# GNN megakernel: the attention layer in 13 parts of 32 edge tiles from one ring of gathered rows

## What is computed

```python
h = (x @ W).reshape(n, 8, 32)
a_src, a_dst = einsum(h, att_src), einsum(h, att_dst)      # n x 8
e = leaky_relu(a_src[src] + a_dst[dst], 0.2)               # edges and one loop per node
m = segment_max(e, dst); e = exp(e - m[dst])
out = segment_sum(h[src] * (e / segment_sum(e, dst)[dst]), dst)
x = layernorm(x + gamma * norm(out + bias) + beta)
```

## Time and profile before

| | us |
|---|---|
| runs shown (3) | 2991.97, 2983.28, 2981.79; median 2983.28 |
| profiled execution, span from first to last instruction | 2974.2 |
| busy: PE, DVE, ACT, POOL | 2470.6, 1396.0, 707.2, 936.7 |

### The profile page before, as it was taken

The page is one execution under the profiler, slowest core; times in us unless marked ns, Lnnn a source line. Parts: engine busy times, 40 slices in busy tenths (PEclk is TensorE's granted clock), DMA queues, the critical chain, the costliest instruction groups (busy, mean ns, idle before and its releaser), DMA issues. The chain is left out here.

```text
span 2974.2 us, 32381 instructions
## 1 busy us (share of the span) xinstructions
PE 2470.6 (83%) x9483; PEld 1621.2 (55%) x9484; DVE 1396.0 (47%) x3940; ACT 707.2 (24%) x1552; POOL 936.7 (31%) x927
## 2 busy tenths in 40 slices
PE   3677789897987999999999999999977886457680
PEld 2444788343766555565556555577743444345560
DVE  7999656455665001030101001455575664546668
ACT  3776545111443000010001000255400000103112
POOL 0000256666666000000000000012167666576740
PEclk9888999998998999999999999999988998678885
DMA  6565678343344743444444434333558887646641
GB/s 233 243 253 225 212 238 264 118 138 97 112 121 137 152 151 129 151 134 151 129 152 133 151 119 145 93 106 102 113 168 271 278 282 245 209 132 190 192 127 43
DMA packets 209534, 493.89 MB, mean 166 GB/s; under 512 B 46457, under 2 KB 128430, under 8 KB 209134
## 3 DMA queue, kind: packets, MB, share of 16 engines
q1 hardware_dynamic: 135185, 301.30, 32.2%
q10 hardware_dynamic: 38173, 133.27, 12.8%
q0 software_dynamic: 36032, 57.60, 7.1%
HBM read 374.71 MB, written 117.32 MB: 165 GB/s over the span
## 5 line engine op out<-in xcount | busy, mean ns | idle before, releaser
L794 POOL DMA_INDIRECT table_dense_weights<-pair_weight,dst x416 | 411.2, 988 | 563.5 <-DVE weights_c L849 324.8
L1526 PE MATMUL banks<-own_term,features_and_rows 128*128 128x391 f32 (+1 forms) x1656 | 552.3, 491 | 0.0
L2134 POOL DMA_INDIRECT features_and_rows<-table_heads,src x376 | 401.7, 1068 | 191.4 <-issue 107.9
L1526 PEld LDWEIGHTS banks<-own_term,features_and_rows 128*128 128x128 f32 x1656 | 312.2, 189 | 226.8
L1552 DVE TENSOR_SCALAR features_and_rows<-banks,hop_bias 128x391 f32<-128x391 f32 (+1 forms) x24 | 15.0, 625 | 762.2 <-PE banks L1526 762.2
L954 PE MATMUL banks<-split_rows,count_columns 128*128 128x512 f32 x1200 | 322.1, 415 | 19.6 <-issue 12.6
L2531 PE MATMUL banks<-features_and_rows,edge_to_window 128*128 x880 | 233.4, 427 | 104.5 <-DVE edge_to_window L2492 71.6
L1526 PE MATMUL banks<-features_and_rows 128*128 128x391 f32 (+1 forms) x840 | 282.4, 491 | 0.0
L954 PEld LDWEIGHTS banks<-split_rows,count_columns 128*128 128x128 f32 x1200 | 226.3, 193 | 76.8 <-issue 21.7
L2531 PEld LDWEIGHTS banks<-features_and_rows,edge_to_window 128*128 128x128 f32 x880 | 181.3, 210 | 156.5 <-issue 122.5
L558 PE MATMUL banks<-features_and_rows,pair_and_bias_rows 128*128 128x400 f16 x806 | 184.3, 388 | 87.1 <-DVE features_and_rows L540 51.9
(11 more groups left out here) (425 smaller groups left out, 3016.8 us busy)
## 6 DMA issues: line engine op xcount, KB each, us to landing
hidden<-table_counts SPq DMA_DIRECT2D x305, 160.0 KB
table_dense_weights<-weights_c ACTq DMA_DIRECT2D x26, 1600.0 KB, 5.7
own_term<-table_dense_weights SPq DMA_DIRECT2D x52, 782.0 KB
features_and_rows<-table_rows_by_edge SPq DMA_DIRECT2D x58, 528.0 KB
own_term<-table_dense_weights SPq DMA_DIRECT2D x34, 780.5 KB
pair_and_bias_rows<-table_edge_rows ACTq DMA_DIRECT2D x50, 512.0 KB
weights_c<-table_edge_rows ACTq DMA_DIRECT2D x50, 512.0 KB
table_rows_by_edge<-features_and_rows SPq DMA_DIRECT2D x48, 528.0 KB
```

The source lines that it names most:

```text
L794: e.indirect_dma_start(out=self.table, out_offset=bass.IndirectOffsetOnAxis(ap=self.place[:, t:t + 1], axis=0), in_=self.values[:, t:t + 1 ...
L1526: m = e.matmul(psum[b][:, 0:wide], z_block(block)[:, f * P:(f + 1) * P], streamed[tile % STREAM][:, lo - from_column:lo - from_column + wi ...
L2134: e.indirect_dma_start(out=to[:, k, :], out_offset=None, in_=t_h, in_offset=bass.IndirectOffsetOnAxis(ap=src[:, t:t + 1], axis=0)).then_in ...
```

## The change

- The 112 scoring stages, the index tables in DRAM, the staging, the write and gather of segment maxima, and the multiplication by own rows in ACT go.
- The head row gets 8 more columns (272 in the ring). The 33rd number of each head is now a_src itself instead of 1, so a gathered row brings its score.
- POOL gathers the 416 tiles in order into a ring of 80 tiles in SBUF, after the two first quads also two fetches of values at the first nodes of scan rows and parts. Then, on POOL too, the own rows are scaled and added to the node sums, in 7 groups of two operations (`add_own`).
- 13 parts of 32 tiles. For each: `prepare`, `weigh`, then `merge_dve`/`merge_pe`, written out instead of in a loop. A scan row is now 2 tiles of one head, so a part's scores are [128, 256]. The exponential is a polynomial on DVE; the weights are turned into PSUM and from there also put into the ring as the 33rd numbers. The own row's exponent comes out of the merge in the 8 new columns, and ACT makes its exponential at each node tile's end.
- A part's scan begins without knowing what follows: what a node that crosses a part bound still has behind it is found in advance. For each of the 12 bounds a round of one POOL fetch of 128 rows of counts (6,400 bytes each) and two DVE operations of 3,200 columns marks the sources of that node (`near_fetch`, `near_counts`), six rounds behind the evictions of hop 0 and six behind those of hop 1, and 12 rounds of small operations with them; a reduction over nodes at the start of the attention gives the bounds' maxima.
- Start values go to one table, one indirect write per node tile instead of two. SP loads dst rows for the scan after the last rows of the third layer, and begins that layer's counts only when the marks are known.
- `wait_loaded` replaces waits on a value from memory: it masks the register first.

The diff, cut to its core:

```diff
+RING_TILES = 80
+RING_AHEAD = 16
+RING_QUADS = RING_TILES // GROUP
+RING_ROW = ATT_ROW + HEADS
+PART_TILES = 32
+PARTS = EDGE_TILES // PART_TILES
+PART_EDGES = PART_TILES * P
...
+        def wait_loaded(e, sem, loaded, bound):
+
+            e.reg_alu(bound, loaded, 511, ALU.bitwise_and)
+            e.wait_ge(sem, bound)
...
-                e.wait_ge(s_zeroed, e.snap(regs[2 * n + 1], min_val=3, max_val=WINDOWS + 2))
+                wait_loaded(e, s_zeroed, regs[2 * n + 1], bound)
...
+        def near_fetch(b, known):
+            def pool(e):
+                if b == 0:
+                    for ready in (*written, known):
+                        e.wait_ge(*ready)
+                else:
+                    e.wait_ge(*near_read[b - 1])
+                e.indirect_dma_start(out=near_rows.rearrange("p k n -> p (k n)"), out_offset=None, in_=t_count,
+                                     in_offset=bass.IndirectOffsetOnAxis(ap=bound_at[:, b:b + 1], axis=0)).then_inc(s_near, 16)
+
+            pr.queue["pool"].append(pool)
+
+        def near_counts(b, ready):
+            t = V(lambda e: e.tensor_scalar(near_hot, iota[:, :], bound_low[:, b:b + 1], None, ALU.is_equal), ready)
+            t = V(lambda e: e.tensor_tensor(near_rows, near_rows, near_hot.unsqueeze(1).broadcast_to([P, NODE_TILES, P]), ALU.mult),
+                  (s_near, 16 * (b + 1)), t)
+            near_read[b] = V(lambda e: e.tensor_reduce(near_penalty[:, b, :], near_rows, AX_X, ALU.add), t)
+            return near_read[b]
...
             e.wait_ge(*w_h)
-            for n in range(STAGED):
-                d = n % DIRECT
-                if n >= DIRECT:
-                    e.wait_ge(s_kept_rows[d], 16 * (n // DIRECT))
-                gather_group(e, STAGED_QUADS[n], staging[d], s_staged[d], GROUP // 2 * n - STAGES_BEHIND)
-                if n == 3:
+            for quad in range(QUADS):
+                if quad >= RING_QUADS:
+                    e.wait_ge(*merged((quad - RING_QUADS) * GROUP + GROUP - 1))
+                for t in range(quad * GROUP, (quad + 1) * GROUP):
+                    e.indirect_dma_start(out=ring_rows[:, ring_at(t), 0:ATT_ROW], out_offset=None, in_=t_h,
+                                         in_offset=bass.IndirectOffsetOnAxis(ap=src[:, t:t + 1], axis=0)).then_inc(s_row[quad % RING_QUADS], 16)
+                if quad == 1:
                     e.wait_ge(*w_pair)
-                    e.wait_ge(*row_first_known)
+                    e.wait_ge(*row_first_in)
                     for c in range(2):
-                        e.indirect_dma_start(out=first_value[:, c:c + 1], out_offset=None, in_=t_pair,
-                                             in_offset=bass.IndirectOffsetOnAxis(ap=row_first[:, c:c + 1], axis=0)).then_inc(s_first_value, 16)
-            gather_direct(e, [q for q in DIRECT_QUADS if q < 2 * IN_CHAIN])
-            gather_direct(e, [q for q in DIRECT_QUADS if 2 * IN_CHAIN <= q < PLACES])
-            gather_last(e)
-            weigh_own(e)
...
+        def add_own(e):
+            for n, g in enumerate(node_groups):
+                rows_of, weights_of = own_rows(g)[:, :, :, 0:HEAD_DIM], tiles(p_self, g)
+                e.wait_ge(s_own_back[g[0] // 16], 16)
+                e.wait_ge(s_summed, g[-1] + 1)
+                e.tensor_tensor(rows_of, rows_of, weights_of.unsqueeze(3).broadcast_to([P, len(g), HEADS, HEAD_DIM]), ALU.mult
+                                ).then_inc(s_own_scaled, 1)
+                e.wait_ge(s_own_scaled, n + 1)
+                sums_of = sum_rows(g)[:, :, :, 0:HEAD_DIM]
+                e.tensor_tensor(sums_of, sums_of, rows_of, ALU.add).then_inc(s_owned, 1)
 
         pr.queue["pool"].append(gather_rows)
-        s_dst_rows = pr.sem("scan_dst_loaded")
...
+        def prepare(b):
+            before = pr.last("dve")
+            seg_made = V(lambda e: e.tensor_tensor(seg[:, 1:], by_dst[:, b, 0:LAST], by_dst[:, b, 1:], ALU.subtract), scaled_dst, before)
+            for c in range(2):
+                held_read[b] = V(lambda e, c=c: e.tensor_tensor_scan(held_in[:, c, :], seg, psum[4][:, c * SCAN_LEN:(c + 1) * SCAN_LEN],
+                                                                     first_value[:, b, c:c + 1], ALU.add, ALU.max),
+                                 held_turned[b], (s_first_value, 32), seg_made)
+            V(lambda e: e.tensor_scalar(begins_here, start_values[b % 2][:, :, :, 0], -0.1 * BIG, None, ALU.is_gt), (s_start[b % 2], 16 * (b // 2 + 1)))
+            V(lambda e: e.tensor_scalar(flags[:, 0, :], by_dst[:, b, :], by_dst[:, b, 0:1], -1.0, ALU.subtract, ALU.mult), scaled_dst)
+            V(lambda e: e.tensor_scalar(flags[:, 1, :], by_dst[:, b, :], by_dst[:, b, LAST:], None, ALU.subtract))
+            for w in range(2):
+                V(lambda e, w=w: e.tensor_scalar(end_mask[:, w, 2 * P:], bound_key, end_key[:, b, w:w + 1], -BIG, ALU.not_equal, ALU.mult))
+                masked_ends[b] = V(lambda e, w=w: e.tensor_scalar(end_mask[:, w, 0:2 * P], keys_of, end_key[:, b, w:w + 1], -BIG,
+                                                                  ALU.not_equal, ALU.mult), keys_spread[b])
+            for j in range(2 * b, min(2 * b + 2, NODE_TILES)):
+                V(lambda e, j=j: e.tensor_tensor(x[:, j, :], x[:, j, :], brow[:, B_BETA, :], ALU.add))
...
+        def turn_scores(b):
+            landed = [row_landed(quad) for quad in part_quads(b)]
+            for lo, hi, at in pieces_of(b):
+                t = V(lambda e, lo=lo, hi=hi, at=at: e.tensor_copy(
+                    in_rows(packed, lo, hi), by_row(ring_rows[:, at:at + hi - lo, HEAD_DIM:ATT_ROW:HEAD_ROW])), *landed)
+            for i in range(SCAN_TILES):
+                m = T(lambda e, i=i: e.transpose(a_turned[:, i * P:(i + 1) * P], packed[:, i, :], ident[:, :]), t, masked_ends[b])
+            return m
+
+        def weigh(b):
+            m = turn_scores(b)
+            t = V(lambda e: e.tensor_tensor(met, a_turned, held_in[:, 1, :], ALU.add), m, held_read[b])
+            t = V(lambda e: e.scalar_tensor_tensor(out=bent, in0=met, scalar=0.2, in1=met, op0=ALU.mult, op1=ALU.max), t)
+            t = V(lambda e: e.tensor_tensor(met, bent, held_in[:, 0, :], ALU.max), t)
+            scanned = V(lambda e: e.tensor_tensor_scan(prefix, seg, met, -BIG, ALU.add, ALU.max), t)
+            V(lambda e: e.tensor_copy(back[:, LAST:], prefix[:, LAST:]), scanned)
+            spread_max = V(lambda e: e.tensor_tensor_scan(back[:, 0:LAST][:, ::-1], seg[:, 1:][:, ::-1], prefix[:, 0:LAST][:, ::-1],
+                                                          prefix[:, LAST:], ALU.add, ALU.max), scanned)
+            for w, at in enumerate((0, LAST)):
+                m = T(lambda e, w=w, at=at: e.matmul(end_values[:, w * P:(w + 1) * P], back[:, at:at + 1].broadcast_to([P, P]), ident[:, :],
+                                                     start=True, stop=True), spread_max)
+            t = V(lambda e: e.tensor_tensor(at_ends, end_mask, all_values.unsqueeze(1).broadcast_to([P, 2, ALL_KEYS]), ALU.add),
+                  m, masked_ends[b], bound_spread)
+            t = V(lambda e: e.tensor_reduce(end_value[:, :], at_ends, AX_X, ALU.max), t)
+            for w in range(2):
+                t = V(lambda e, w=w: e.scalar_tensor_tensor(out=back, in0=flags[:, w, :], scalar=end_value[:, w:w + 1], in1=back,
+                                                            op0=ALU.add, op1=ALU.max), t)
+            of_tiles = lambda to, i: to.rearrange("p (r i) h -> p i r h", i=SCAN_TILES)[:, i, :, :]
+            for i in range(SCAN_TILES):
+                max_turned = T(lambda e, i=i: e.transpose(of_tiles(max_of, i), back[:, i * P:(i + 1) * P], ident[:, :]), t)
+            gap = met
+            t = V(lambda e: e.tensor_tensor(gap, bent, back, ALU.subtract), t)
+            t = V(lambda e: e.tensor_scalar(power, gap, LOG2_E, -126.0, ALU.mult, ALU.max), t)
+            t = V(lambda e: e.tensor_scalar(rounded, power, ROUNDER, None, ALU.add), t)
+            scaled = V(lambda e: e.tensor_scalar(scale_i.bitcast(I32), rounded, ROUNDER - 127.0, float(1 << 23), ALU.subtract, ALU.mult), t)
+            t = V(lambda e: e.scalar_tensor_tensor(out=rest_of, in0=rounded, scalar=ROUNDER, in1=power, op0=ALU.subtract, op1=ALU.subtract), t)
+            t = V(lambda e: e.tensor_scalar(power, rest_of, EXP2[-1], None, ALU.mult), t)
+            for k in range(len(EXP2) - 2, 0, -1):
+                t = V(lambda e, k=k: e.scalar_tensor_tensor(out=power, in0=power, scalar=EXP2[k], in1=rest_of, op0=ALU.add, op1=ALU.mult), t)
+            t = V(lambda e: e.scalar_tensor_tensor(out=gap, in0=power, scalar=EXP2[0], in1=scale_i, op0=ALU.add, op1=ALU.mult), t, scaled)
+            for i in range(SCAN_TILES):
+                m = T(lambda e, i=i: e.transpose(of_tiles(weight_of, i), gap[:, i * P:(i + 1) * P], ident[:, :]), t)
+            own_gap = by_tile(rounded)
+            begins = start_values[b % 2][:, :, :, 0]
```

(38 more changed lines are left out.)

863 lines of the change are left out of this document (303 added, 560 removed).

## The result

Beside the kernel before on one chip (2987.2 us, median of 4), the changed kernel takes 3035.1 us (3027.8 to 3039.2, 4 runs): ratio 1.0148, 95% interval 1.0116 to 1.0180. It is slower by 1.5%, where 2875 us and faster had been forecast. The profiled execution's span is 3035.4 us against the 2866.2 of the sum. First the head of the page, and its chain by engine.

A forecast was written before the change was run, and what follows sets the result against it. Waits set the pace before; after the change POOL's gathers would. 2186.5 + 552.5 + 2.7 + 15.7 + 29.3 + 71.5 + 8 = 2866.2 us span, with 9.1 more 2875 us; range 2837 to 2936, 8 in 10.

The forecast's parts named there:

- Item 1: Start of POOL's gathers: stays at 2186.5 us, behind the last write of head rows.
- Item 2: POOL's 418 gathers and first-value fetches: 522.5 us plus 30 of stretching, 552.5 us in all, 42.5 per part of 32.
- the stretching: Gathers made longer beside DVE instructions with both inputs in SBUF: 30 us taken, bounds 0 and 50.
- the 24 of its working: Stretching beside the small SBUF operations of 12 parts, 1.9 us each: 24 us, with 6 more for set-up beside part 0.
- Item 3: DVE's chain in a part of the merge stretch: 38.6 us, under POOL's 42.5, so POOL is the bound.
- merge 18.0: Merge of a part's eight quads by DVE and PE, about two of them slow: 18.0 us of the part's 38.6.
- Item 4: After the last gather: landing 2.7 us, last part 15.7 and 29.3, last norm and rest to the span's end 71.5.
- Item 5: Own rows scaled and added on POOL near the end: 8 us taken, bounds 0 and 24.6.
- Item 6: Before 2186 us: twelve nearest-source rounds of 15 us fit DVE's idle time in the hops, cost 0; bounded waits also 0.
- The 9.1 us: Added to the summed span: the distance of the three runs' median, 2983.28 us, above the profiled span of before.
- A: Rival: DVE's chain bounds each part at P of 44 to 50 us; chance 0.25, including gathers that don't come free.
- The signs set for being wrong: The prediction is wrong if POOL's last gather comes after 2800 or the last norm starts after 2860.

The follow-up runs named there:

- e1: Changed kernel with the merge's matmuls reporting once in four steps instead of every step: 3016.7 us, ratio 1.0127 to the kernel before.
- e12: Changed kernel in its own order, with six small products of POOL after every 4 gathers: 3058.7 us, single run.
- e13: Changed kernel, next part weighed while one is merged, SP's 16 target-number transfers behind the table's last writes: 2744.2 us beside 2804.3, ratio 0.9791.
- e17: Changed kernel as it is, timed again beside the kernel before: 2765.5 us against 2802.7, ratio 0.9868.
- e16: Kernel before with bounded waits, POOL waiting after every 8 gathers for landed rows once the merge has begun: 2846.5 us beside 2804.3, ratio 1.0146.

## Why the prediction was wrong

- *Item 1, the start*: 2205.9, not 2186.5. 4.4 us go with hops that end 4.9 us later in this execution (1921.6 against 1916.7 for their last matmul; in e1 to e12 they end at 1900.4 to 1913.0, so this part isn't the change's), 15.0 from SP: "the start stays at 2186.5, behind the last write of head rows" counted POOL's queue and not SP's, on which 16 transfers of target numbers are moved ahead of the last two writes. e13 shows it (0.3 us). In e1 to e12 this wait is 12.3 to 16.8 us.
- *Item 2, gathers at 552.5 us*: right where TensorE isn't held up: 536.7 in e17 (418 x 1.25 is 522.5, and 8.8 are waits for PE; the stretching was 5, not 30; the 24 of its working are 22.8 by their own factors, 12 x 1.9). In the first profile 693.5.
- *Item 3, "POOL is the bound; DVE has 3.9 us spare"*: the failed step. The chain was sized roughly right, even too long (35.3 us without gathers, 38.6 forecast), and in e17 DVE waits 7.1 us a part for rows. But "merge 18.0" took PE's blocks at their recorded pace beside 24 gathers in a row, and two stalls of 11 and 5.5 us came on top. The part became 53.3 us long, DVE had nothing spare, and POOL waited for PE's merge (129.9 us put down to it, 42.3 more to "remote").
- The error behind it is in the first paragraph: the chain's 8.66 us on "another core or an unknown queue" were read as transfers of staged rows, so they were expected to go with staging. They were PE's late reports, in a merge beside gathers, the one thing that the change keeps and puts under every part. The trace of before says so: the piece starts the idle time of these one-hots, which wait for PE's count alone, and the matmuls that they need stand as done at 2590.74, 19.5 us earlier, while POOL issues 25 gathers in a row (L2453, the maxima).

```profile
2609.13 0.94 POOL L2453 DMA_INDIRECT tmp<-table_running_max,row_of_last_edge  x1 [0.30 <-issue]
2610.23 0.69 DVE L2492 TENSOR_TENSOR edge_to_window<-banks,dst_of_step 128x512 f32<-128x512 f32 x1 [12.20 <-issue]
```

  In e16, which keeps the staging, the merge's one-hots wait "remote" not at all, against 64.6 us before. Its pauses alone can't be the reason: the scoring stage, where it has none, lost its 42.7 us of such waits as well.
- *Item 4, the end*: 136.0 (129.1 in e17) for 127.2. The last part's first copy comes 6.6 us behind the last gather's end, not 2.7, and not because a row landed late: DVE has no idle time ahead of it, as it still merged and prepared. The last norm took 75.6 instead of 71.5. *Item 5, own rows*: 11 us where 8 were taken (below).
- *Item 6*: the near rounds fit, as forecast; from the first eviction to the last matmul the hops take 796.6 us, not 794.3.
- *The 9.1 us* put on top of the sum are no offset. The profiled execution's time is 3037.5 for a span of 3035.4, 2.1 us apart; the 9.1 was the distance of one execution from the median of others, and here it is -0.3. Against the sum's 2866.2 the miss is 169.2 us, against the 2875 only 160.
- *The rivals*: A (DVE's chain the bound, P 44 to 50, with a time of 2359.6 + 12 P) had the right place of the wait, POOL on PE, and by its formula P = 53.3 gives 2999; what is missing is the start and part 0. Its cause was another. The range (to 2936) was too narrow since no rival let a wait of before stay. That TensorE could be late for a reason outside both kernels' code was in none of them, nor could one trace show that the same kernel takes 172 us less elsewhere. The signs set for being wrong did come: the last gather starts at 2898.5, not before 2800, and the last norm at 2959.7, not before 2860.

## What to carry to other kernels

A wait that the trace puts on "another core" in a kernel of one core is a fact to be explained, not a transfer to be assumed: look what else runs whenever it appears, before pricing a change that keeps it. A change that packs one engine's bursts beside another's runs can lose to one that breaks them up: pauses of 2 us on POOL won 1.8%, an order that spreads PE's work 2.7%, both where the hold-up exists. And where two conditions turn the sign of a ratio, time against the old kernel in each.
